# Masking the second pass of a graph attention block on GpSimd, with adjacency tiles in the x buffers

## The reference

```
h = maximum(layernorm(x), 0)                     # x: (16, 512, 512) float32
q, k, v = heads(h @ Wq + bq), heads(h @ Wk + bk), heads(h @ Wv + bv)
scores = einsum('bhqd,bhkd->bhqk', q, k) / sqrt(32)
scores = where(adj[:, None] == 0, -inf, scores)  # adj: (16, 512, 512) int32, mostly 0
attn = softmax(scores, axis=-1)
out = x + einsum('bhqk,bhkd->bhqd', attn, v) @ Wo + bo
```

## Time and profile before

| | |
|---|---|
| time, median of 3 runs | 1778.74 us (1775.16 to 1779.21) |
| span of the profiled execution | 1774.9 us |
| time of the profiled execution around its span | not recorded; the median is 3.8 us above the span |
| PE busy | 1702.4 us, 96% |
| DVE busy | 1450.9 us, 82% |
| ACT busy | 1447.0 us, 82% |
| POOL busy | 140.8 us, 8% |
| TensorE clock granted | full in every slice of the page |

### The profile page before, as it was taken

The page is one execution under the profiler, slowest core; times in us unless marked ns, Lnnn a source line. Parts: engine busy times, 40 slices in busy tenths (PEclk is TensorE's granted clock), DMA queues, the critical chain, the costliest instruction groups (busy, mean ns, idle before and its releaser), DMA issues.

```text
span 1774.9 us, 32235 instructions
## 1 busy us (share of the span) xinstructions
PE 1702.4 (96%) x8129; PEld 1040.2 (59%) x8256; DVE 1450.9 (82%) x3493; ACT 1447.0 (82%) x3397; POOL 140.8 (8%) x200
## 2 busy tenths in 40 slices
PE   3889999999999999999999999999999999999997
PEld 2646666665666556665666656656566665666643
DVE  5778888888888888888888888888888888888783
ACT  2688888887888888888888878888788888888884
POOL 0000100000000011100000000001100001010010
...
GB/s 166 112 85 109 97 103 86 111 89 105 109 92 111 82 113 109 96 102 83 111 91 105 110 90 108 88 113 107 99 98 86 113 91 107 110 95 96 84 61 36
DMA packets 118720, 175.64 MB, mean 99 GB/s; under 512 B 32385, under 2 KB 34433, under 8 KB 118529
## 3 DMA queue, kind: packets, MB, share of 16 engines
...
q10 hardware_dynamic: 4096, 1.06, 0.3%
...
## 4 chain that ended last, share of the span: by engine, by line
PE 88%; DVE 4%; ACT 2%; issue 2%; SPq 2%; DMA 1%; POOL 0%; ACTq 0%; DVEq 0%; POOLq 0%
PE ps L723 16%; PE psO L754 14%; PE psP L647 14%; PE ps L734 13%; PE psP L649 12%; PE psP L648 12%; PE ps L737 5%; PE ps L695 2%; ACT ps L397 1%; DVE x_tile L468 1%; PE ps L701 1%; DVE ps L544 1%; SPq L270 1%; SPq L266 1%; SPq L273 1%
## 5 line engine op out<-in xcount | busy, mean ns | idle before, releaser
L544 DVE CUSTOM_DVE_ANT_0 ps<-ps,bias_q 128x512 f32<-128x512 f32 x1024 | 710.9, 696 | 243.9 <-PE ps L723 229.3
L397 ACT ACTIVATE ps<-ps,neg_max 128x512 f32<-128x512 f32 x1024 | 681.8, 666 | 125.8 <-DVE neg_max L544 85.4
L427 ACT ACTIVATE probs<-ps 128x512 f32<-128x512 f32 x1024 | 614.8, 601 | 88.9 <-PE ps L734 78.8
L723 PE MATMUL ps<-k_stack,q_stack 96*128 96x512 f32 x1024 | 449.7, 439 | 20.4 <-ACT ps L397 11.4
L734 PE MATMUL ps<-q_stack,k_stack 98*128 98x512 f32 x1024 | 409.8, 401 | 4.0 <-ACT probs L427 3.3
L551 DVE SCALAR_TENSOR_TENSOR probs<-bias_k,probs 128x512 f32<-128x512 bf16 x512 | 363.3, 710 | 12.7 <-ACT probs L427 12.7
L723 PEld LDWEIGHTS ps<-k_stack,q_stack 96*128 96x128 f32 x1024 | 192.8, 188 | 270.1 <-ACT ps L397 132.3
L754 PE MATMUL psO<-probs,v_sb 128*32 128x512 f32 x2048 | 274.4, 608 | 2.7 <-DVE probs L551 1.5
L734 PEld LDWEIGHTS ps<-q_stack,k_stack 98*128 98x128 f32 x1024 | 195.1, 191 | 44.0 <-ACT probs L427 17.1
L397 ACT ACTIVATION_READ_ACCUMULATOR ps<-ps,neg_max 128x1 f32 x1024 | 209.0, 204 | 0.0
L737 PE MATMUL ps<-bias_k,ident_b 128*128 128x512 bf16 x385 | 151.1, 392 | 0.0
...
## 6 DMA issues: line engine op xcount, KB each, us to landing
q_stack<-part_hi SPq DMA_DIRECT2D x512, 64.0 KB, 2.0
k_stack<-part_hi SPq DMA_DIRECT2D x512, 64.0 KB, 2.0
x_tile<-in_x_dram SPq DMA_DIRECT2D x64, 256.0 KB, 2.8
adj_tile<-in_adj_dram SPq DMA_DIRECT2D x64, 256.0 KB, 2.9
...
y_tile<-in_x_dram SPq DMA_DIRECT2D x64, 256.0 KB, 2.7
out_dram<-y_tile SPq DMA_DIRECT2D x64, 256.0 KB, 2.1
```

The lines of the kernel that those rows point to most:

```text
L397: nc.scalar.activation(item, item, ACT.Exp, scale=-1.0, bias=neg_max[:, g % 2, col:col + 1], accum_out=exp_sum[:, g % 2, col:col + 1]).the ...
L427: nc.scalar.activation(probs[:, n % P_RING, :], ps2[:, n % 2, :], ACT.Exp, scale=SCALE).then_inc(exp2_done, 1)
L544: nc.vector.tensor_tensor_reduce(bank1(("s", u)), bank1(("s", u)), bias_q[:, qt, :], -SCALE, 3.0e38, ALU.add, ALU.min, neg_max[:, g % 2, c ...
L723: nc.tensor.matmul(bank1(("s", u)), q_stack[0:STACK, g, j, P * qt:P * qt + P], k_stack[0:STACK, g, j, :], start=True, stop=True).then_inc( ...
```

## The change

The added matmul (L737) and DVE's masking (L551) both go. All 64 exponentials of a graph (16 heads by four tiles of keys) are masked on GpSimd, two at a time: the 128x1024 exponentials are read as int32 and multiplied with int32 values of 0 or 1 from `keep_k`, which one instruction on DVE makes out of the transposed mask. There are 32 such multiplications in a block, at every odd n. The multiplication with v now waits for these, and stands a slot later (u % 4 == 3), and so does the evacuation of `psO`; the last of them moves to slots 1 and 2 of the next block, and the output projection waits for it only at its last quarter.

`keep_k` takes twice the room of `bias_k`, and several buffers shrink or are shared. The one that matters for the order: `adj_tile` is gone, and adjacency tiles are loaded into the two halves of `x_tile`. So x tiles 0 and 1 of the next graph can be loaded only when the adjacency tiles 2 and 3 have been used; their loads move from u = 12 and 15 to u = 34 and 38, and the uses of adjacency move earlier. Last, the loop and its registers are gone: all 19 blocks are written out.

```diff
-ADJ_AT = (17, 24, 30, 36)
-BIAS_AT = (24, 30, 36, 46)
+ADJ_AT = (14, 16, 25, 31)
+BIAS_AT = (24, 28, 32, 37)
...
-O_HI_AT = {16: 0, 31: 1, 47: 2, 63: 3}
-O_LO_AT = {17: 0, 32: 1, 48: 2, 63: 3}
+O_HI_AT = {1: (3, -2), 16: (0, -1), 32: (1, -1), 48: (2, -1)}
+O_LO_AT = {2: (3, -2), 17: (0, -1), 33: (1, -1), 49: (2, -1)}
...
+        def adj_view(t):
+            return x_tile[:, t % 2, :].bitcast(I32)
...
-                    sp.wait_ge(h_turned, due(4 * b + t - 1))
+                    if t >= 2:
+                        sp.wait_ge(h_turned, due(4 * b + t - 1))
+                    else:
+                        sp.wait_ge(bias_done, due(4 * (b - 1) + t + 3))
                     sp.dma_start(x_tile[:, t % 2, :], x_rows[bass.ds(row, 1)].rearrange("a p d -> (a p) d")
                                  ).then_inc(x_in[t % 2], 16)
 
...
-                    sp.wait_ge(bias_done, due(4 * b + t))
-                    sp.dma_start(adj_tile[:], adj_rows[bass.ds(row, 1)].rearrange("a p d -> (a p) d")
-                                 ).then_inc(adj_in, 16)
+                    if t < 2:
+                        sp.wait_ge(h_turned, due(4 * b + t + 3))
+                    else:
+                        sp.wait_ge(bias_done, due(4 * b + t - 1))
+                    sp.dma_start(adj_view(t), adj_rows[bass.ds(row, 1)].rearrange("a p d -> (a p) d")
+                                 ).then_inc(adj_in[t % 2], 16)
...
+                    if k == 0 and u == 2: load_weight("v", Wv)
+                    if k == 0 and u == 6: load_weight("o", Wo)
+                    if u == 34: load_x(k + 1, 0)
+                    if u == 38: load_x(k + 1, 1)
                     if u in ADJ_AT: load_adj(k, ADJ_AT.index(u))
...
+            def mask(b, n):
+                if n == 1:
+                    pool.wait_ge(m_done, due(2 * b + 1))
+                if n == 9:
+                    pool.wait_ge(m_done, due(2 * b + 2))
+                pool.wait_ge(exp2_done, due(64 * b + n + 1))
+                at = (n - 1) % P_RING
+                pair = probs[:, at:at + 2, :].bitcast(I32)
+                keep = keep_k[:, n % 16 // 4, :].unsqueeze(1).broadcast_to([P, 2, S])
+                nc.gpsimd.tensor_tensor(pair, pair, keep, ALU.mult).then_inc(probs_masked, 1)
+
             def step(k, parity):
-                form_rstd(k, 2)
-                add_bo(k - 2, 2)
-                form_rstd(k, 3)
-                add_bo(k - 2, 3)
-                for t in range(2):
-                    form_rstd(k + 1, t)
-                if known(k) and k == 0:
-                    pool.wait_ge(small_in, 64)
-                for t in range(2):
-                    add_bo(k - 1, t)
-
-            blocks(pool, step, counters=[(next_aggr, 4 * LOOP_FROM + 3)])
+                for u in range(SLOTS):
+                    if u == 5: form_rstd(k, 2)
+                    if u == 9: add_bo(k - 2, 2)
+                    if u == 10: form_rstd(k, 3)
+                    if u == 13: add_bo(k - 2, 3)
+                    if u == 41: form_rstd(k + 1, 0)
+                    if u == 43: form_rstd(k + 1, 1)
+                    if k == 0 and u == 49: pool.wait_ge(small_in, 64)
+                    if u in (50, 52): add_bo(k - 1, (u - 50) // 2)
+                    b, n = pass2(k, u)
+                    if have(b) and n % 2 == 1:
+                        mask(b, n)
+
+            blocks(step)
...
                     dve.wait_ge(m_turned, due(2 * b + n + 1))
-                    dve.wait_ge(scores2, due(64 * (b - 1) + 48 + 8 * n + 8))
-
-                    dve.wait_ge(probs_masked, due(MASKED_ALL * (b - 1) + masked_before(48 + 8 * n + 8)))
-                    nc.vector.tensor_copy(bias_k[:, 2 * n:2 * n + 2, :], bank1((kind, n, rel)).bitcast(BF16).rearrange("p (t q) -> p t q", q=S)
-                                          ).then_inc(m_done, 1)
+                    dve.wait_ge(probs_masked, due(32 * (b - 1) + 24 + 4 * n + 4))
+                    nc.vector.tensor_scalar(keep_k[:, 2 * n:2 * n + 2, :],
+                                            bank1((kind, n, rel)).bitcast(BF16).rearrange("p (t q) -> p t q", q=S),
+                                            0.0, None, ALU.is_equal).then_inc(m_done, 1)
                 else:
...
-                    b, n = pass2(k, u - 1) if u else pass2(k - 1, SLOTS - 1)
-                    if have(b) and n % 8 in VECTOR_MASKED:
-
-                        dve.wait_ge(exp2_done, due(64 * b + n + 1))
-                        nc.vector.scalar_tensor_tensor(out=probs[:, n % P_RING, :], in0=bias_k[:, n % 16 // 4, :], scalar=-MASKED,
-                                                       in1=probs[:, n % P_RING, :], op0=ALU.add, op1=ALU.min
-                                                       ).then_inc(probs_masked, 1)
                     if u in C_AT:
...
-                        if g == 0 and j == 0:
-                            pe.wait_ge(m_done, due(2 * b + kt // 2 + 1))
                         pe.wait_ge(exp2_done, due(64 * b + n - 1))
-                        last = nc.tensor.matmul(ps2[:, n % 2, :], k_stack[:, g, j, P * kt:P * kt + P], q_stack[:, g, j, :],
-                                                start=True, stop=(n % 8 in VECTOR_MASKED))
-                        if n % 8 not in VECTOR_MASKED:
-                            last = nc.tensor.matmul(ps2[:, n % 2, :], ident_b[:], bias_k[:, kt, :], start=False, stop=True)
-                        last.then_inc(scores2, 1)
+                        nc.tensor.matmul(ps2[:, n % 2, :], k_stack[:, g, j, P * kt:P * kt + P], q_stack[:, g, j, :],
+                                         start=True, stop=True).then_inc(scores2, 1)
                     project(k, u)
-                    if u % 4 == 2 and have(k - 1):
+                    if u % 4 == 3 and have(k - 1):
...
-                        pe.wait_ge(exp2_done, due(64 * b + 4 * n + 4))
-                        pe.wait_ge(probs_masked, due(MASKED_ALL * b + masked_before(4 * n + 4)))
+                        pe.wait_ge(probs_masked, due(32 * b + 2 * n + 2))
```

More of the change, by code:

```diff
@@ L196, in pass2, with blocks @@
             return (k, u - S2_AT) if u >= S2_AT else (k - 1, u + SLOTS - S2_AT)
-        def masked_before(n):
-            return n // 8 * len(VECTOR_MASKED) + sum(i < n % 8 for i in VECTOR_MASKED)
-        MASKED_ALL = masked_before(SLOTS)
-        def blocks(eng, block, first=-1, counters=()):
-            for k in range(first, LOOP_FROM):
-                block(k, k % 2)
-            for counter, value in counters:
-                counter.start(value)
-            with eng.Fori(LOOP_FROM, LOOP_TO, 2) as k:
-                block(k, 0)
-                block(k + 1, 1)
-            for k in range(LOOP_TO, B + 2):
-                block(k, k % 2)
+        def adj_view(t):
+            return x_tile[:, t % 2, :].bitcast(I32)
+        def blocks(step, first=-1):
+            for k in range(first, B + 2):
+                step(k, k % 2)
         block = ctx.enter_context(nc.Block())
@@ L381, in step @@
                 for u in range(SLOTS):
[L382 removed]
+                    if k == 0:
                         if u in SPLIT_AT:
@@ L759, in step @@
                             turn(k, kind, n, rel)
-            pe.wait_ge(ident_done, 4)
-            blocks(pe, step)
+            pe.wait_ge(ident_done, 3)
+            blocks(step)
 _INS = ['x', 'adj', 'L0_gnn_Wq', 'L0_gnn_bq', 'L0_gnn_Wk', 'L0_gnn_bk', 'L0_gnn_Wv', 'L0_gnn_bv', 'L0_gnn_Wo', 'L0_gnn_bo']
```

126 lines of the change are left out of this document (46 added, 80 removed).

## The result

| | before | after |
|---|---|---|
| median of 4 runs, us | 1778.04 | 1931.98 (1923.98 to 1942.52) |
| ratio with its interval | | 1.0861 (1.0822 to 1.0901) |
| profiled span, us | 1774.9 | 1940.7 |
| a block, mean of the fourteen full ones, us | 106.4 | 115.9 |

The changed kernel is 8.6% slower; 1793 us was predicted, with 1865 as the upper end. Of the span's 165.8 us, 132.7 lie in the fourteen full blocks, 23.5 ahead of them and 9.6 behind them.

What follows compares the result with a forecast made beforehand. PE, busy 96% of the span, was taken as the bound. 97.5 + 5.1 + 3.8 + 0.4 + 0.5 less 0.2 made 107.1 us a block against 106.4; with the ends, 1793 us, range 1720 to 1865.

Steps and rivals of the forecast that it cites:

- the floor: PE's work in a block without the 32 masking matmuls and without any wait: 105.05 - 7.5 = 97.5 us.
- The loop's turn: A 2.64 us issue piece in the chain, taken as part of the 1.36 us of waits already left out.
- the multiplication: POOL's masking instruction on 128x1024, 32 in a block: 2.4 us each, POOL at 85.6 us a block.
- the rival of the slow multiplication: POOL's multiplication takes 3.2 us and POOL bounds the kernel at 114.7 us a block: 1900 us, chance 0.10.
- slot 13: Late y tile, rstd and a POOL multiplication winning the port delay DVE's normalisation; PE waits 5.1 us, 3.1 if DVE wins.
- the late x tile: Slot 42: x tile 1's load stands behind k's set of group 1; DVE stands still 5 us, PE loses 3.8.
- I take 0.5 us a block: Loss from DVE's other 20 SBUF-to-SBUF instructions in a block, most thought to fall in POOL's 1 us gaps.
- three ring banks: Cover between DVE's standstills and PE, claimed to be enough for a standstill of 2.4 us.
- The constants in slot 52 lose the port three times: Rival: with POOL behind, DVE stands still 6 us and more, 5.5 us a block more: 1870 us, chance 0.12.
- the copy of the transposed mask: DVE's copy, twice a block, may double with its wider output; nothing waits at it.
- The sum: Per block 97.5 + 5.1 + 3.8 + 0.4 + 0.5 less 0.2: 107.1 us against 106.4, +10 us in fourteen blocks.
- The ends: Outside the full blocks: block 1 -3 us, block 0 +4 us, the kernel's end +3.5 us.

Runs made afterwards that it cites:

- e9: After with constants on GpSimd, x loads a slot earlier, additions at slots 58 and 60, rstd first, and the first mask transpose back in slot 53: 1682.76 us.
- e1: Before with its loop written out and nothing else: 1767.31 us, 0.9932.
- e6: After with POOL's rstd of t = 3 ahead of its addition to y tile 2: 1893.25 us, 1.0641.
- e2: Before, loop written out, with adjacency in the x buffers and loads and uses placed as in after; masking stays on PE and DVE: 1840.27 us, 1.0333.
- e7: After with four moves: constants on GpSimd, x loads a slot earlier, additions at slots 58 and 60, rstd of t = 3 first: 1701.56 us, 0.9553.
- e3: After with the three softmax-constant instructions moved from DVE to POOL, where they are four: 1848.73 us, 1.0386.
- e8: After with only the first 256 of each head's 512 columns multiplied, the other half's mask left out: 1821.83 us, 1.024.
- e10: e7 with the softmax constants back on DVE: 1793.57 us, 1.0085.
- e4: After with the loads of x tiles 0 and 1 one slot earlier, at 33 and 37: 1899.27 us, 1.0692.
- e5: After with POOL's two bias-row additions moved from slots 50 and 52 to 58 and 60: 1848.37 us, 1.039.
- e11: e7 with POOL's additions back at slots 50 and 52: 1702.10 us, 0.9566.

## Why the prediction was wrong

**Nearly right: the floor.** I had 97.5 us of work a block without the masking matmuls; e9 has 98.3 and 1.0 of waits. The 0.8 us of work above it were not traced. The loop's turn, which this floor had left out already, was worth 0.95 us by e1.

**Right: the multiplication.** 2.4 us predicted, 2.39 measured. POOL never became the bound, and the rival of the slow multiplication is out.

**Right in kind, too large: slot 13.** The mechanism is the one predicted, shown by the timeline above and by e6. PE waits 2.2 us more there than in e9, where I had 5.1, and loses 3.3 in all, the rest being slow matmuls. The y tile left SP at 577.33, +15.1 from the block's opening, and not at the +17.3 that I took from the earlier trace rows, so POOL added it sooner and was at the rstd at +21.1.

**Right in kind: the late x tile.** SP's path came as predicted: in the block shown the load had landed at +39.5 from slot 20's opening and slot 46 opened at +42.1, where I had +38.9 and +41.5. e2, where nothing stands in front of it, loses 4.6 us in slots 45 to 47 where I had 3.8. That the two are near is partly luck: PE waits 2.2 us there, less than forecast, and the other 2.4 us are busy time at the low clock, for which I had nothing. In after the place costs 1.9 against e9, as DVE comes to the tile late.

**The step that failed: "I take 0.5 us a block" for DVE's instructions with SBUF at both ends.** I had 20 such instructions and let most of them fall in gaps of POOL. But POOL multiplies 76 of 116 us, and where it is behind it goes from one instruction to the next without a gap. So the 20 instructions cost DVE 16.4 us a graph, slot 13's included, and beside slot 13 PE sees of it 3.0 us in slots 36 to 44, 4.9 in slots 52 to 55 and 2.0 in slots 56 to 59 (after less e7), the clock included. That is 9.9 us for 0.5: 5.3 of waits and 4.6 of longer busy time. The cover that I named, three ring banks for 2.4 us of a standstill, is enough for one loss alone: slot 20 has one of 1.24 us on average and the adjacency goes on losing about 0.9 us in e9, and PE hardly waits for either (0.0 us in slots 16 to 35, 0.1 in slots 36 to 44 of e9). It isn't enough where losses follow closely, as at slot 36 (2.2 us and, 1.4 us later, 1.3 for the adjacency) and at slot 52 (three in a row). e3 shows it by taking the constants away, e8 by making each hold shorter, e10 by bringing them back alone.

The Trainium skill, "SBUF — State Buffer", SBUF: two separate sides, says of a VectorE instruction with two SBUF inputs or in a 2-port mode, and a GpSimd instruction that reads SBUF, that whichever of the two starts first gets the pair of ports for its whole instruction, and that the other fully blocks. The rows of slot 52 agree: L442 and L447, with two SBUF inputs each, take 2.37 and 2.27 us and alone 0.17. I knew the rule, used it once, at slot 13, and did not go through the other instructions with it.

**The rival that happened.** "The constants in slot 52 lose the port three times" describes 651.19 to 657.03 as it came, for 5.5 us a block and 1870 us, with a chance of 0.12. Its condition, a backlog of two additions, stood in the order of POOL's program, and could have been followed like slot 13. It misses the constants in slot 36 and the clock.

**Not in the prediction at all: PE's clock.** e9 and after issue the same matmuls, and after is busy 105.2 us a block for 98.3. The 6.9 us are matmuls at 1.2 GHz, 42% of the 16.5 us a block between the two; a granted clock of 0.94 over 115.9 us makes the same 6.9. In the full blocks of the trace before PE never stood still for long and the clock was 1.00. But block 1 of that trace shows the price, and I did not read it: PE waits 2.25 us at 105.34 and 0.97 at 108.05, and then (columns as above)

```profile
108.00:113.00 5.00, 4.57 (x16) 2.27 (x18) 2.47 (x6) 2.73 (x7) 0.00 (x0) 0.50 0.27 105
```

So a standstill should have been priced with slow matmuls behind it, or the range widened for them.

**A term put at nothing: the copy of the transposed mask.** The prediction let it double and wrote that nothing waits at it. It takes 1220 ns for 684, and from slot 55 on, where the change put its transpose, PE waits for it: 16.4 us in e7, and moving it back takes 1.3 us a block from slots 56 to 59 (e9).

**The sum.** Against e9 a block of after has 3.3 (slot 13) + 3.0 (36 to 44) + 1.9 (x tile) + 4.9 and 3.3 (slot 52 and behind it, 1.3 of it the mask's turn) + 0.2 elsewhere, 16.5 us before rounding. The prediction had 9.8 of such losses. How much of each place is waits of PE and how much longer busy time can be read by windows over each place in both traces (us a block, after less e9):

| | 13-15 | 36-44 | 45-47 | 52-55 | 56-59 | elsewhere | sum |
|---|---|---|---|---|---|---|---|
| waits | 2.2 | 1.9 | 1.2 | 4.2 | 0.2 | 0.0 | 9.7 |
| busy | 1.0 | 1.2 | 0.8 | 0.6 | 3.1 | 0.2 | 6.9 |

The ends were off too: +23.5 us ahead of the full blocks, where I had +1, and +9.6 behind them, where I had +3.5. In e4 block 0 ends 10 us sooner than in after, which is the late x tile again, and in e9 the full blocks start 8.1 us before those of the kernel before.

Two slips in the working change nothing: 41.5 less 37.6 is 3.9 us and not 3.8, and the 2.8 us at which POOL's rate would bound is that of a block of 97.5 us without the waits.

Single edits don't add up to their sum. e3, e4, e5 and e6 alone gain 83, 33, 84 and 39 us, together 238; in e7 they gain 230. That looks like addition and isn't: e5's gain is worth nothing beside e3 (e11), and the late x load, 33 us alone, hides more behind the constants (6.54 to 10.86 us in e3). What stays open: what decides whether the clock falls (in slots 36 to 44 PE waits 2.0 us in each of the fourteen blocks, and the clock is low for a part of these slots in eight of them), and why DVE is behind POOL by 0.05 to 0.13 us at so many of these meetings, was not tried.
